# Five of sixteen tiles over ScalarE and GpSimd in a Mamba and mixture-of-experts layer

## The reference

```
# block 1: bidirectional Mamba; ED = 512 channels, N = 16 states, one direction d:
xz = x @ W_in.T ;  u = silu(conv4(xz[..., :ED])) ;  z = xz[..., ED:]
dbc = u @ Wx.T  ->  delta = softplus(dbc[..., :64] @ Wdt.T + b_dt), B (16), C (16)
h[t, e, n] = exp(delta[t, e] * A[e, n]) * h[t-1, e, n] + delta[t, e] * B[t, n] * u[t, e]
y[t, e]    = sum_n h[t, e, n] * C[t, n] + D[e] * u[t, e]
out = ((y_forward + y_backward) / 2 * silu(z)) @ W_out.T
# block 2: 8 experts (256 -> 512 -> 256, gelu), the best 2 by a softmax router, and one shared expert
```

## Time and profile before

| what | value |
|---|---|
| median of 3 runs | 4417.94 us (4411.51 to 4418.87) |
| span of the profiled execution | 4422.2 us |
| TensorE, VectorE, ScalarE, GpSimd busy | 81%, 86%, 70%, 79% |
| VectorE adds, GpSimd adds | 1488, 496 |

### The profile page before, as it was taken

How to read it: one execution, slowest core, us unless ns; L and a number is a source line. 1 busy time by engine, 2 the same in 40 slices (tenths; PEclk the granted TensorE clock), 3 DMA queues, 4 the chain that set the end, 5 groups by cost and what they waited for, 6 DMA issues and landing times.

```text
span 4422.2 us, 57941 instructions
## 1 busy us (share of the span) xinstructions
PE 3604.0 (81%) x18192; PEld 2562.9 (58%) x18192; DVE 3788.5 (86%) x4688; ACT 3101.8 (70%) x5179; POOL 3504.8 (79%) x2085
## 2 busy tenths in 40 slices
PE   4767596888879887798878887798987989788877
PEld 1444454666546655567555774556655665567656
DVE  3999999898998989899898988989999898989710
ACT  4667576787767876688766887678876787668543
POOL 3898887888878888788887888878887888878611
PEclk7878697999979999899879998899998999889988
DMA  6233142556435663357433674345743565336555
GB/s 196 91 107 104 69 150 75 191 183 214 155 104 172 205 210 130 105 182 245 153 124 131 197 238 147 125 151 194 230 141 107 179 220 188 130 113 204 167 167 182
DMA packets 375805, 705.06 MB, mean 159 GB/s; under 512 B 31937, under 2 KB 205514, under 8 KB 371530
## 3 DMA queue, kind: packets, MB, share of 16 engines
q1 hardware_dynamic: 363210, 667.79, 46.0%
q0 software_dynamic: 12288, 33.57, 2.3%
HBM read 529.82 MB, written 171.44 MB: 159 GB/s over the span
## 4 chain that ended last, share of the span: by engine, by line
DVE 29%; PE 25%; POOL 16%; issue 15%; ACT 11%; DMA 3%; SPq 1%; DVEq 0%; POOLq 0%; ACTq 0%
DVE h L1396 10%; POOL drive L1895 9%; DVE h L1393 7%; DVE y L1405 6%; PE h_t L1170 5%; PE side L1204 4%; PE side L1341 4%; PE side L1333 3%; ACT decay L1610 2%; POOL y L1913 2%; POOL xs_dram L1970 2%; DMA expert_w<-in_w 1%; PE side L1318 1%; DVE stats L1450 1%; POOL work L1982 1%
## 5 line engine op out<-in xcount | busy, mean ns | idle before, releaser
L1895 POOL TENSOR_TENSOR drive<-xu,b_row 128x1024 f32<-128x1024 f32 x960 | 2262.7, 2362 | 386.5 <-DVE h L1396 238.8
L1610 ACT ACTIVATE decay<-delta,neg_a 128x512 f32<-128x512 f32 x2048 | 1401.8, 692 | 747.0 <-DVE h L1396 424.5
L1170 PE MATMUL h_t<-ident,h 128*128 128x128 f32 x8192 | 1332.0, 301 | 523.4 <-DVE y L1405 253.4
L1170 PEld LDWEIGHTS h_t<-ident,h 128*128 128x128 f32 x8192 | 1060.1, 155 | 979.1 <-DVE y L1405 373.1
L1405 DVE SCALAR_TENSOR_TENSOR y<-h_t,c_col,y 128x512 f32<-128x512 f32 x1488 | 1085.9, 730 | 54.0 <-PE h_t L1170 52.9
L1913 POOL TENSOR_TENSOR y<-y,scaled 128x512 f32<-128x512 f32 x496 | 631.8, 1274 | 119.4 <-ACT scaled L1631 118.4
L1396 DVE TENSOR_TENSOR_SCAN h<-decay,h,drive 128x512 f32<-128x512 f32 x512 | 654.1, 1278 | 38.6 <-ACT decay L1610 18.6
L1396 DVE TENSOR_TENSOR_SCAN h<-decay,drive 128x512 f32<-128x512 f32 x512 | 622.0, 1215 | 71.9 <-ACT decay L1610 45.8
L1393 DVE TENSOR_TENSOR_SCAN h<-decay,h,drive 128x512 f32<-128x512 f32 x448 | 573.1, 1279 | 44.7 <-ACT decay L1610 23.1
L1393 DVE TENSOR_TENSOR_SCAN h<-decay,drive 128x512 f32<-128x512 f32 x448 | 544.5, 1215 | 76.4 <-POOL drive L1895 55.7
L1204 PE MATMUL side<-prep_work,conv_diag 128*128 128x512 f32 x960 | 460.9, 605 | 27.3 <-DMA prep_work<-xz_dram 19.3
(11 more groups left out here) (205 smaller groups left out, 4355.7 us busy)
## 6 DMA issues: line engine op xcount, KB each, us to landing
expert_w<-in_w SPq DMA_DIRECT2D x350, 512.0 KB, 4.5
b_row<-b_dram SPq DMA_DIRECT2D x240, 512.0 KB, 4.2
x_dram<-xu SPq DMA_DIRECT2D x16, 2048.0 KB, 7.6
delta_dram<-prep_work SPq DMA_DIRECT2D x64, 512.0 KB, 2.9
delta<-delta_dram SPq DMA_DIRECT2D x64, 512.0 KB, 4.9
ys_dram<-work SPq DMA_DIRECT2D x40, 512.0 KB, 6.5
work<-xs_dram SPq DMA_DIRECT2D x38, 512.0 KB, 4.4
h<-in_w SPq DMA_DIRECT2D x34, 512.0 KB, 5.5
```

Source lines behind the costliest of these rows:

```text
L1170: t = pe.e.transpose(h_t[i % N_H_T][:, c * P:(c + 1) * P], its_h[:, c, :], ident[:, :])
L1610: act.e.activation(decay[:, i % N_DECAY, :], delta[:, c, its], ACT.Exp, scale=neg_a[:, c, w % 2, n:n + 1]).then_inc(decay_made, 1)
L1895: op = pool.e.tensor_tensor(drive[:, k % N_DRIVE, :], xu[:, w % 2, c, :], b_row[:, row % N_B_ROW, :], ALU.mult)
```

## The change

The tiles that go over ScalarE and GpSimd are five of sixteen in place of four. All numbers of `AT` and `BANK_USE` are replaced. `PARTS` is 256 in place of 16, with slots numbered as before. The transfers of SP all lie in slots -140 to -136, one after the other. The two first expert weights, `b1_load` and `zero_store` get places of their own. No instruction is different in kind, and no wait is added to a piece.

```
-POOL_TILES = (2, 6, 10, 14)
+POOL_TILES = (1, 4, 7, 10, 13)
-PARTS = 16
+PARTS = 256
+FIRST_EW = (-35805, -35804)
+B1_AT = -35806
+ZERO_AT = -35808
 AT = {
-    "tok_load": [-2240, -2239, 1440, 1696, 5200, 5632, 9168, 9649, 13345, 13824, 17392, 17921, 21632, 22000, 25744,
...
 BANK_USE = {
...
     for i in range(2):
-        plan.put("sp", 0, "ew_load", i)
+        plan.put("sp", FIRST_EW[i], "ew_load", i)
...
-    plan.put("sp", 0, "b1_load")
-    plan.put("sp", 0, "zero_store")
+    plan.put("sp", B1_AT, "b1_load")
+    plan.put("sp", ZERO_AT, "zero_store")
```

## The result

| | after | before, same chip | ratio, 95% interval |
|---|---|---|---|
| first measurement | 4395.5 us (4390.9 to 4400.5, 4 runs) | 4418.4 | 0.9951 [0.9936, 0.9967] |
| repeated later, as c_after | 4404.2 us (4398.5 to 4415.3, 12 runs) | 4418.9 | 0.9974 [0.9964, 0.9984] |

The change makes the kernel faster, by 22.9 us and then by 14.7 us, where 43 us were predicted. The sign is right and the size is about half, then a third. The experiments show that the sign came out of two large terms, of which the prediction had one with the wrong sign and the other at zero.

The account below looks back on a forecast made before the run. VectorE was taken to lead in 45 of 67 windows, TensorE in 17, GpSimd in 5. Window gain 50.7 us less 8 us for drive waits gave 43, other terms 0: 4418 to 4375 us, range 4328 to 4430.

Parts of the forecast that it names:

- step 5: All places anew: side work shifts by a median 0 to 2 slots; 63 us either way, taken as 0.
- Step 3: 67 windows of 60 us, each shrinking or growing as its highest engine does: 50.7 us of gain in sum.
- The first reading of the waits: VectorE's waits inside the scan loop are short, 145 us in 4422, so over long stretches it has no gaps.
- Step 4: GpSimd's slack of 383 us takes 153 us more work; later drives cost VectorE 8 us, bounds 0 and 80.
- The GpSimd rival: GpSimd becomes the bound around scatters and gathers, VectorE's drive waits double by 80 us: 4447 us, chance 0.17.
- Step 7: The tail behind the last scan: only the order counts, same chain of products; 0, 5 us either way.
- Step 6: The head: zero fill's 12.00 us of issuing moves ahead of the second delta_store; taken as 0, ends -14 and +12.
- Steps 1 and 2: VectorE 1.00 us lighter per sixteen slots, 121 us if it bound everywhere; GpSimd gets 153 us more, ScalarE 81.
- TensorE-led windows as long as before: Sign expected in the profile after: the windows in which TensorE leads keep their length.
- tens of us: Sign that would make the forecast wrong: VectorE's waits for decays grow by tens of us.
- the gain is eaten: Rival: TensorE and routing joins set each batch's length, VectorE waits longer for h_t or decay; 4409 to 4427, chance 0.12.

Follow-up runs that it names:

- e1_share: The kernel before with only POOL_TILES changed to (1, 4, 7, 10, 13), all places as before: 4464.1 us, ratio 1.0104.
- e3_odd4: The kernel before with POOL_TILES = (1, 5, 9, 13), still four tiles of sixteen, on the old places: 4479.7 us, ratio 1.0146.
- f3_both: The kernel after with both edits, the spread scatters of f1_spread and the later products of f2_bank: 4411.4 us, ratio 0.9987.
- x_ kernels: ScalarE scales its tile ahead of the decay in each slot: kernel before 4426.1 us, before with new share on old places 4502.1 us, kernel after 4435.3 us.
- f1_spread: The kernel after with the sixteen scatters of batch 0 and of batch 4 spread over more slots: 4409.3 us, ratio 0.9982.
- f2_bank: The kernel after with six of TensorE's side products a slot or two later, every engine's order unchanged: 4409.7 us, ratio 0.9978.

## Why the prediction was half right

**Two steps failed together, 3 and 5.** The first is step 5, the places ("I take 0 and keep a third of it, 20 us, for the range"). With the new share, the places were worth 60 to 69 us (e1_share against after), as much as the +-63 us that the step itself had worked out. It counted pieces that hurt and pieces that help as if they cancelled, from the shift of each kind, one to two slots. The shift is the wrong measure. e3_odd4, in which no place shifts at all and four tiles stand in other slots, costs 63 us. The likeliest reading is that whether a place fits depends on which slots the tiles load.

**Step 3 is the other.** It took the windows' 50.7 us of gain as there whatever the places are, and let each window shrink as its busiest engine does. With the places kept, the share costs 47 us where it counted 43 of gain. If work were free to move inside 60 us, e3_odd4, in which no engine has more to do, would have had to be no slower. Chains such as the one from ScalarE over a bank of h_t to TensorE and VectorE (3.12 and 5.69 us at 2044 us of e1_share) are shorter than a window, and busy sums don't show them. That the two errors, of some 90 and 60 to 69 us, cancel to the right sign is luck.

**The first reading of the waits was short.** "The three largest rows of VectorE that name the loop come to 145 us" leaves out the waits for a turned tile, 52.9 us, and one of the two rows for decays, 43.8, both larger than the third that it took. All of them come to 257 us, 6% of the span. These two kinds are the ones that grew.

**Step 4 had the wrong sign.** It charged 8 us for later drives; the waits for drives fell from 91 to 82 us, those of L1384 and its like counted in. The GpSimd rival (4447 us) failed with it.

**Step 7, the tail at 0 within 5 us:** 266.3 us became 252 to 255. This is 11.0 of the 32.5 us between the profiles of before and after, 13.7 of 19.8 with c_after, and it is there in every kernel on the new places (251.8 to 255.9, but for f3_both's 260.7); on the old ones the tail is 261.7 to 272.1. The traces show part of where: behind the last scan the router's logits start at 79.5 us before and at 74.0 after, and the last gathers at 227.4 and 216.5. Which exchange in the tail brings it was not tried.

**Step 6, the head at 0:** right in its sum. First scan 8 us sooner, 0.3 us by slot 16. The zero fill's issuing takes 2.42 us now, not 12.00, with the stall for the decay 11.26 us for 14.55.

**Steps 1 and 2:** right in the counts, in GpSimd's 3643 us for 3658, and in 0.9 us for 1.00 in sixteen slots. VectorE's "about 3668, level" is off: it is busy 3701 us. The step took 121 us between starts off a sum of busy times, where 120 adds of 0.73 us are 88. "TensorE-led windows as long as before" was wrong: slots 128 to 143 went from 28.2 to 31.5 us and slots 400 to 415 from 29.9 to 26.0, since the new places move TensorE's work between them. The decay waits grew by "tens of us", one of the signs named beforehand.

**Against the rival "the gain is eaten" (4409 to 4427):** its mechanism, VectorE waiting longer for h_t and decays, is what the trace shows, 53 to 91 us and 108 to 132 us, though the time stayed below its range.

**What stays open.** Of the 47 us of the share on the old places 28 remain with a light ScalarE. TensorE still waits 66 us there for scaled tiles against 25 in its partner, so ScalarE's order, not only its time, is a candidate, but that is argued and not shown: the one order tried in its place, in the x_ kernels, was worse. A fourth bank for h_t would test it and wasn't tried. What the new places do right was not found as a rule either; the two that I read out of the tables (no bunched scatters, no product ahead of its bank) are broken by the faster kernel, and the mending tried gains nothing.

## What to carry to other kernels

A schedule written out by hand belongs to the loads that it was fitted to: price a change of share and a refit of the places as two terms, never the second at nothing because its average shift is small. Windows of busy time gave no more than an upper bound here on what easing an engine brings. Chains shorter than a window decide how much of it arrives; add up all waits of the leading engine, row by row, before and after. A stall in the trace is worth its length only if what stands behind it isn't waiting for something else: of 22.6 us of stalls aimed at in f1_spread and 23.5 us in f2_bank, nothing reached the end.

## What the runs showed of the hardware that was not expected

- TensorE's granted clock can be raised by idle work (0.895 to 0.928 on the mean, with more of the time at 2.4 and less at 1.2 GHz) with no time gained, 14 us lost. A lower clock in the slower of two kernels need not be its cause. In single places it does cost: 24 steps of one product took 7.88 us at a clock of 0.68 and 5.35 at 1.00.
- The same kernel, profiled twice: spans 4389.7 and 4402.4 us, clocks 0.901 and 0.896. Many stretches of 16 slots agree to 0.1 us, and single ones differ by 2 to 5.
- ScalarE's scaling of 64 columns takes 0.30 us, of 512 0.675: a fixed part of about a quarter of a microsecond, by the line through both.
- GpSimd issues an indirect scatter in 0.96 us with 0.30 between, but a gap of 2.13 and 2.14 us stands ahead of the fifteenth of sixteen in both bunches of after, and one of 2.14 in batch 3, where they come spread. What it waits for isn't shown.
